# Splitting the next weights of an MoE feed-forward stage ahead of the phase and expert boundaries

## What is computed

```python
# x: (4, 2048, 1024); w1: (8, 1024, 2048); w2: (8, 2048, 1024)
xf = x.reshape(-1, D)
...
norm_g = masked / (masked + 1e-06)          # one number per token
h = gelu(einsum('nd,edh->neh', xf, w1) + b1)
y = einsum('neh,ehd->ned', h, w2) + b2
out = (y * norm_g[:, None, None]).sum(axis=1)
```

## Time and profile before

| what | us |
|---|---|
| device time, median of 2 runs | 10499.08 (10113.11 and 10885.05) |
| device time of the profiled execution | 10143.3 |
| its span on the slowest core (core 0) | 10141.3 |
| spans of the 8 cores | 10066.1 to 10141.3 |
| TensorE (matmul) busy | 8027.9, 79% of the span |
| ScalarE busy | 3868.2, 38% |
| VectorE busy | 2731.3, 27% |

### The profile page before, as it was taken

How to read it: one execution, slowest core, us unless ns; L and a number is a source line. 1 busy time by engine, 2 the same in 40 slices (tenths; PEclk the granted TensorE clock), 3 DMA queues, 4 the chain that set the end, 5 groups by cost and what they waited for, 6 DMA issues and landing times. The chain is left out here.

```text
span 10141.3 us, 83716 instructions; the slowest of 8 cores (10066.1 to 10141.3 us)
## 1 busy us (share of the span) xinstructions
PE 8027.9 (79%) x30908; PEld 3836.4 (38%) x31404; DVE 2731.3 (27%) x4507; ACT 3868.2 (38%) x3688; POOL 7.5 (0%) x15
## 2 busy tenths in 40 slices
PE   4585678898885677898896777889887676898898
PEld 2253433333332433333332333333333333343343
DVE  2213112333332112333333112333333112333332
ACT  1112003565563003565553003556554102555554
POOL 0000000000000000000000000000000000000000
PEclk7555578999997677999997667999998666999998
DMA  1000012222221111222221111222221111222222
GB/s 45 0 0 27 33 56 77 86 91 88 87 92 39 40 67 69 90 88 88 91 87 43 46 67 54 90 87 90 88 88 54 50 67 40 87 94 83 88 94 98
DMA packets 207024, 696.36 MB, mean 69 GB/s; under 512 B 29088, under 2 KB 30120, under 8 KB 206624
## 3 DMA queue, kind: packets, MB, share of 16 engines
q1 hardware_dynamic: 202048, 673.27, 19.0%
q0 software_dynamic: 4576, 17.71, 0.5%
HBM read 682.51 MB, written 8.39 MB: 68 GB/s over the span
## 5 line engine op out<-in xcount | busy, mean ns | idle before, releaser
L1172 PE MATMUL ps<-XNFH,W1SH 128*128 128x512 bf16 x4012 | 1552.8, 387 | 371.0 <-DVE W1SL L1130 363.7
L1219 PE MATMUL ps<-W2SH,H1FH 128*128 128x512 bf16 x4012 | 1559.3, 389 | 199.0 <-DVE W2SL L1151 193.9
L1174 PE MATMUL ps<-XNFL,W1SH 128*128 128x512 bf16 x4012 | 1550.3, 386 | 61.0 <-DVE W1SL L1130 56.6
L1222 PE MATMUL ps<-W2SL,H1FH 128*128 128x512 bf16 x4016 | 1560.1, 388 | 5.5 <-issue 1.4
L1229 PE MATMUL ps<-W2SH,H1FL 128*128 128x512 bf16 x4012 | 1557.0, 388 | 4.2
L1176 PE MATMUL ps<-XNFH,W1SL 128*128 128x512 bf16 x4016 | 1552.4, 387 | 5.1 <-issue 0.9
L1143 ACT ACT_TABLE_LOAD x512 | 656.9, 1283 | 1412.9 <-PE ps L1229 1411.7
L1151 DVE TENSOR_TENSOR W2SL<-W2SF,W2SH 128x1024 bf16<-128x1024 f32 x512 | 627.1, 1225 | 1984.9 <-ACT W2SH L1143 1984.9
L1187 ACT ACT_TABLE_LOAD x512 | 656.9, 1283 | 1122.9 <-PE ps L1176 1122.9
L734 PE MATMUL ps<-WSLAB,XNF 128*128 128x512 f32 x1536 | 802.9, 691 | 208.2 <-DMA WSLAB<-wq 70.1
L1172 PEld LDWEIGHTS ps<-XNFH,W1SH 128*128 128x128 bf16 x4096 | 405.4, 99 | 1060.5 <-issue 647.4
(11 more groups left out here) (180 smaller groups left out, 5004.9 us busy)
## 6 DMA issues: line engine op xcount, KB each, us to landing
W1SF<-w SPq DMA_DIRECT2D x512, 512.0 KB, 3.5
W2SF<-w SPq DMA_DIRECT2D x512, 512.0 KB, 3.5
WSLAB<-wv SPq DMA_DIRECT2D x64, 512.0 KB, 3.8
WSLAB<-wg SPq DMA_DIRECT2D x64, 512.0 KB, 3.8
WSLAB<-wo SPq DMA_DIRECT2D x64, 512.0 KB, 3.7
WSLAB<-wq SPq DMA_DIRECT2D x64, 256.0 KB, 2.7
WSLAB<-wk SPq DMA_DIRECT2D x64, 256.0 KB, 2.6
X<-x POOLq DMA_DIRECT2D x1, 8192.0 KB, 28.8
```

The costliest lines, as they stand in the source:

```text
L1172: t.matmul(ps[:, ab: ab + 512], B["W1SH"][:, half + dc * 128: half + dc * 128 + 128], XH[:, dc * 512:(dc + 1) * 512], start=(dc == 0), sto ...
L1174: t.matmul(ps[:, ab: ab + 512], B["W1SH"][:, half + dc * 128: half + dc * 128 + 128], XL[:, dc * 512:(dc + 1) * 512], start=False, stop=False)
L1219: t.matmul(ps[:, yb: yb + 512], B["H1FH"][:, hsl], B["W2SH"][:, half + dh * 512: half + dh * 512 + 512], start=(hc == 0), stop=False)
L1222: t.matmul(ps[:, yb: yb + 512], B["H1FH"][:, hsl], B["W2SL"][:, half + dh * 512: half + dh * 512 + 512], start=False, stop=False)
```

## The change

The two splitting helpers become functions of the whole stage, with their waits as arguments, and four calls move. The first two splits of w2 are emitted in phase A, behind steps 12 and 13. The first two splits of the next expert's w1 are emitted in phase B of the expert before, behind its steps 14 and 15, and so ahead of the additions into X; the waits on TensorE's no-operation go. An expert that is the first of its block has its w1 splits where they were. Because the order of the splits is no longer one phase after the other, the counts of `wvs` that TensorE and SP wait for are worked out in two tables, `w1v` and `w2v`, and the last two of the expert before are kept in `c.lw1` and `c.lw2`. The number and the shape of all instructions stay as they were.

```diff
+    def w1split(hc, dma_wait, ts_wait, val):
+        @blk.scalar
+        def _(s, hc=hc):
+            s.wait_ge(*dma_wait)
+            s.wait_ge(*ts_wait)
...
+        @blk.vector
+        def _(v, hc=hc):
+            v.wait_ge(wcs, c.wc)
...
-        wv0 = c.wv
+        W0 = c.wv
+        w1v, w2v = {}, {}
+        if pend is None:
+            w1v[0], w1v[1] = W0 + 1, W0 + 2
+            i = W0 + 2
+        else:
+            w1v[0], w1v[1] = W0 - 1, W0
...
             for hc in range(16):
-                e2.wait_ge(wvs, max(0, (wv0 - 17 + hc) if hc < 2 else (wv0 + hc - 1)))
+                e2.wait_ge(wvs, w1v[hc - 2] if hc >= 2 else c.lw1[14 + hc])
...
-        w1split(0)
-        w1split(1)
+        if pend is None:
+            w1split(0, w1_dma[0], (tsem, a_ts0), w1v[0])
+            w1split(1, w1_dma[1], (tsem, a_ts0), w1v[1])
+        pend = None
         for hc in range(16):
             @blk.tensor
-            def _(t, hc=hc, e=e, wv0=wv0):
-                t.wait_ge(wvs, wv0 + hc + 1)
+            def _(t, hc=hc, e=e, w1v=w1v):
+                t.wait_ge(wvs, w1v[hc])
...
             if hc + 2 < 16:
-                w1split(hc + 2)
-
-        w2split(0)
-        w2split(1)
+                w1split(hc + 2, w1_dma[hc + 2], (tsem, a_ts0 + hc + 1), w1v[hc + 2])
+            if hc == 12:
+                w2split(0, w2_dma[0], (ybs, c.lyb), w2v[0])
+            if hc == 13:
+                w2split(1, w2_dma[1], (ybs, c.lyb), w2v[1])
+
         for hc in range(16):
...
             if hc + 2 < 16:
-                w2split(hc + 2)
+                w2split(hc + 2, w2_dma[hc + 2], (tsem, b_ts0 + hc + 1), w2v[hc + 2])
+            if e < 7 and hc in (14, 15):
+                hcn = hc - 14
+                dw = (sqab[hcn], (c.sqa if hcn == 0 else c.sqb) + 16)
+                w1split(hcn, dw, (tsem, a_ts0 + 15 + hcn), c.wv + 1)
```

More of the change, by code:

```diff
@@ L75, in __init__ @@
         self.wv = 0
+        self.lw1 = {i: 0 for i in range(16)}
+        self.lw2 = {i: 0 for i in range(16)}
+        self.lyb = 0
 def build_program(upto="full", dbg=()):
@@ L1071, in l1_ffn_tt, with w2split, _ @@
     wcs, wvs = B["wcs"], B["wvs"]
+    ybs = B["ybs"]
+    pend = None
[4 more added lines that the diff above has]
+            s.wait_ge(*ts_wait)
+            half = (hc % 2) * 1024
+            s.copy(B["W1SH"][:, half: half + 1024],
+                   B["W1SF"][:, half: half + 1024]).then_inc(wcs, 1)
+            c.wc += 1
+        @blk.vector
+        def _(v, hc=hc):
+            v.wait_ge(wcs, c.wc)
+            half = (hc % 2) * 1024
+            v.tensor_tensor(B["W1SL"][:, half: half + 1024],
+                            B["W1SF"][:, half: half + 1024],
+                            B["W1SH"][:, half: half + 1024],
+                            ALU.subtract).then_inc(wvs, 1)
+            c.wv += 1
+            assert c.wv == val, (c.wv, val)
+    def w2split(hc, dma_wait, rd_wait, val):
+        @blk.scalar
+        def _(s, hc=hc):
+            s.wait_ge(*dma_wait)
+            s.wait_ge(*rd_wait)
+            half = (hc % 2) * 1024
+            s.copy(B["W2SH"][:, half: half + 1024],
+                   B["W2SF"][:, half: half + 1024]).then_inc(wcs, 1)
+            c.wc += 1
+        @blk.vector
+        def _(v, hc=hc):
+            v.wait_ge(wcs, c.wc)
+            half = (hc % 2) * 1024
+            v.tensor_tensor(B["W2SL"][:, half: half + 1024],
+                            B["W2SF"][:, half: half + 1024],
+                            B["W2SH"][:, half: half + 1024],
+                            ALU.subtract).then_inc(wvs, 1)
+            c.wv += 1
+            assert c.wv == val, (c.wv, val)
     for e in range(8):
@@ L1082, in l1_ffn_tt, with _ @@
         b_ts0 = a_ts0 + 16
-        wv0 = c.wv
+        W0 = c.wv
[5 more added lines that the diff above has]
+            w1v[0], w1v[1] = W0 - 1, W0
+            assert (w1v[0], w1v[1]) == tuple(pend["vals"]), (w1v, pend)
+            i = W0
+        for g in range(16):
+            if g + 2 < 16:
+                i += 1
+                w1v[g + 2] = i
+            if g == 12:
+                i += 1
+                w2v[0] = i
+            if g == 13:
+                i += 1
+                w2v[1] = i
+        for g in range(14):
+            i += 1
+            w2v[g + 2] = i
         w1_dma, w2_dma = [], []
         @blk.sync
-        def _(e2, e=e, wv0=wv0):
+        def _(e2, e=e, w1v=w1v, w2v=w2v):
             for hc in range(16):
-                e2.wait_ge(wvs, max(0, (wv0 - 17 + hc) if hc < 2 else (wv0 + hc - 1)))
+                e2.wait_ge(wvs, w1v[hc - 2] if hc >= 2 else c.lw1[14 + hc])
                 sem = sqab[hc % 2]
@@ L1102, in _ @@
             for hc in range(16):
-                e2.wait_ge(wvs, max(0, (wv0 - 1 + hc) if hc < 2 else (wv0 + 15 + hc)))
+                e2.wait_ge(wvs, w2v[hc - 2] if hc >= 2 else c.lw2[14 + hc])
                 sem = gqab[hc % 2]
@@ L1114, in _ @@
                     w2_dma.append((sem, c.gqb))
[L1116 to L1155, removed]
+        if pend is not None:
+            assert w1_dma[0] == pend["dma"][0] and w1_dma[1] == pend["dma"][1], \
+                (w1_dma[:2], pend)
         ss0 = c.ss
         vs0 = c.vs
-        w1split(0)
-        w1split(1)
+        if pend is None:
+            w1split(0, w1_dma[0], (tsem, a_ts0), w1v[0])
+            w1split(1, w1_dma[1], (tsem, a_ts0), w1v[1])
+        pend = None
         for hc in range(16):
             @blk.tensor
-            def _(t, hc=hc, e=e, wv0=wv0):
-                t.wait_ge(wvs, wv0 + hc + 1)
+            def _(t, hc=hc, e=e, w1v=w1v):
+                t.wait_ge(wvs, w1v[hc])
                 if hc == 0 and e > 0:
@@ L1232, in _ @@
                         if hc == 15 and tc == 2 and dh == 1:
-                            ii.then_inc(B["ybs"], 1)
+                            ii.then_inc(ybs, 1)
                             c.yb += 1
                 if hc == 15:
-                    ii.then_inc(B["ybs"], 1)
+                    ii.then_inc(ybs, 1)
                     c.yb += 1
@@ L1242, in l1_ffn_tt @@
             if hc + 2 < 16:
-                w2split(hc + 2)
+                w2split(hc + 2, w2_dma[hc + 2], (tsem, b_ts0 + hc + 1), w2v[hc + 2])
[3 more added lines that the diff above has]
+                w1split(hcn, dw, (tsem, a_ts0 + 15 + hcn), c.wv + 1)
+                if hcn == 0:
+                    pend = {"dma": [dw], "vals": [c.wv]}
+                else:
+                    pend["dma"].append(dw)
+                    pend["vals"].append(c.wv)
+        c.lw1 = w1v
+        c.lw2 = w2v
+        c.lyb = c.yb
         @blk.vector
         def _(v, tt=tt):
-            v.wait_ge(B["ybs"], c.yb - 1)
+            v.wait_ge(ybs, c.yb - 1)
             for tc2, dh in ((2, 0), (2, 1)):
@@ L1255, in _ @@
             c.vs += 1
-            v.wait_ge(B["ybs"], c.yb)
+            v.wait_ge(ybs, c.yb)
             for tc2, dh in ((3, 0), (3, 1), (0, 0), (0, 1), (1, 0), (1, 1)):
```

4 lines of the change are left out of this document (2 added, 2 removed).

## The result

The changed kernel is faster: its time over that of the kernel before is 0.970, with a 95% interval of 0.962 to 0.978.

What follows compares the result with a forecast made beforehand. TensorE, busy 79% of the span, and its pauses were taken as the bound: 10143.3 - 179 - 73 - 22 - 32 = 9837 us, named as 9830 for a run timed lower, range 9760 to 9925.

Steps and rivals of the forecast that it cites:

- the last of the sum: Whole kernel: 9837 us by the profiled execution, some 30 us less if timed as the lower run; 9830 named.
- Expert to expert, pauses: Phase B to next expert's phase A: the 6.5 us pause goes but for 0.1; 6.4 x 28 = 179 us.
- Rival (3): Experts' boundary: additions behind two subtractions hold TensorE; a 2.4 us slip gives back 67 us, total 9904; chance 0.09.
- Expert to expert, clock: Behind experts' boundaries: with no pause the clock stays at 1.00; 2.6 x 28 = 73 us gained.
- Phase A to phase B, pauses: Boundary 2.4 us shorter, new pause ahead of step 15 costs 1.9; 0.7 x 32 = 22 us gained, ends +29 and -43.
- Rival (2): Phase A's end: ScalarE waits for w2 loads, so the pause moves without shrinking; 43 us lost, total 9934; chance 0.10.
- Phase A to phase B, clock: Behind the boundary's shorter 3.7 us pause: less low clock, 1.0 us each, 32 us gained, ends 0 and 80.
- the row with 4.32 us: Trace row, idle 4.32 us ahead of the matmul at 1316.11 ended at clock 0.50; nearest case, saying the clock falls.
- Rival (1): Clock at the phase change: as it was, 9869; never low, 9789; within the forecast's own 0.76 chance.
- the w1 part: Next expert's early w1 splits at the experts' boundary: 179 us of pauses and 73 of clock.
- the w2 part: Early w2 splits at phase A to phase B: 22 us of pauses and 32 of clock.
- Rival (4): Feed-forward: denser matmuls bring granted clock 0.81; on half of it 620 us more, total 10457; chance 0.03.

Runs made afterwards that it cites:

- Only the w1 part: Changed kernel with the first two w2 splits back ahead of phase B; feed-forward 5920 us (5904 in the changed kernel), fastest timed execution 9843.8 us.
- only the w2 part: Changed kernel with the next expert's first two w1 splits back behind the additions into X; feed-forward 6190 us, profiled execution 10084 us.
- w2 loads earlier: Changed kernel with loads of w2 slices 0 and 1 issued ahead of w1 loads for steps 14 and 15; feed-forward 5878 us, timed 9789.6 and 9796.9.
- the densest kernel: Changed kernel with w1 copy ahead of Gelu, phase B's first step reordered, w2 splits behind steps 13 and 14; ratio to before 0.926, best 9382.1 us.
- w2 splits two steps later: Changed kernel with the first two w2 splits behind steps 14 and 15 instead of 12 and 13; feed-forward 5840 us, die 1 cores 9703 to 9713 us.
- phase B's order: Changed kernel, w2 splits behind steps 13 and 14, phase B's first step in chunk order 3, 0, 1, 2, `H1FL` wait moved; feed-forward 5656 us, ratio to before 0.945.

## Why the prediction was right, and where it was not

**The number against the medians.** The forecast of the time is wrong: 9830 us, range 9760 to 9925, against a median of 10528 over all executions. The step that failed is the last of the sum, the level that the saving is taken from: "if the changed kernel is timed as the lower run was, some 30 us less are to be expected. I name 9830". The working had two timed runs before it, 7.6% apart, and took the lower for the one that counts; nothing in the profile said so. The runs showed the other level: ten executions of the kernel before have a median of 10493.7, where the two on the table had 10499.1. Even from there the ratio would have given 10182, 3% under the 10528 measured, so over all executions together the gain does not show (1.003). What the profile supports is the ratio of like executions: 9837 / 10143.3 = 0.970, and 0.970 was measured. The sum, 9837 us, is 0.3% over what the profiled execution after took, and the four times that the result names for the changed kernel (9775 to 9861) lie in the range.

**Expert to expert, pauses: 179 us forecast, 179 measured.** Every step of it holds, down to the order of what is late next: the second subtraction, then the pair of additions, which holds TensorE for 0.07 us at the place shown (0.1 forecast). Rival (3), that the additions hold TensorE, is out: its group has 0.5 us ended by X in the whole run.

**Expert to expert, clock: 73 forecast.** The 2.6 us of one fall come from the stretch at 0.50 in the earlier trace rows (13 matmuls in 5.24 us). "Only the w1 part" measures 76 in phase A. What I left out is what this does elsewhere: the low stretches behind the pauses at the phase change, which the edit does not touch, became shorter, 30 us more. The term was priced place by place. Why one change shortens the low stretches at another place is open (see below).

**Phase A to phase B, pauses: 22 forecast, 12 to 14 measured.** (80 won ahead of B; 68 given back within A in "only the w2 part", 66 in the kernel after.) The working had the mechanism: an instruction put into a queue with 0.57 us of slack. The size of the new pause was 2.0 us instead of 1.5 to 1.9 in the mean, because the load was late in 21 places of core 0, 19.9 us in all. Rival (2), the load late everywhere, is out as a whole case (at 6.8 us everywhere it had 43 us lost), but in part it holds; "w2 loads earlier" takes 26 us of it back.

**Phase A to phase B, clock: 32 forecast, 7 measured** in "only the w2 part" (26 won, 19 lost). The clock falls behind the pause of 3.56 us at most places (240 of 256 there, 217 of 256 in the kernel after), as the row with 4.32 us said; what I took for the chance that it does not, 1.0 us of 2.5, was about right in phase B (123 x 0.21 / 32 = 0.8). But I had not asked what the new pauses of 2 to 3.5 us inside phase A do to the clock, and they cost most of it again. Rival (1) had its ends at 0 and 80; the truth lies near the first.

So the sum came out right (306 us forecast, 304 measured in the feed-forward) by luck, because two errors met: the w1 part was sized 36 us too small (252 for 288), the w2 part 36 too large (54 for 18). That shows only in the two single experiments, not in the result.

**What ScalarE's queue cost.** The 1.28 us of the table load are there again, ahead of every copy and every Gelu, and next to no time stands between: the table load of a Gelu starts 0.02 us behind the end of the copy before it (2583.16 + 1.04 = 2584.20, next load 2584.22). So the inserted copy held the queue for 2.36 us (2581.86 to 2584.22), where the working had 2.35. With the w2 load in time the pause ahead of step 15 is 1.37 us, where the working had 1.5.

**Rival (4), a lower granted clock in the feed-forward.** Not seen as an effect of the change: the feed-forward parts show 0.98 or 0.99 for 0.96 before, and in the densest kernel, the last of the experiments, core 0 has 1.00 with TensorE busy for 500.00 of 500.00 us. Two things limit this. Cores 6 and 7 of that same execution show 0.99 from 4500 to 5000 us, and their feed-forward took 5459 and 5467 us for the median of 5425. And the level of the rival does occur in a feed-forward part; core 0 of "w2 splits two steps later", a core that is not in the account:

```profile
4500.00:5000.00 500.00, 489.33 (x1855) 201.51 (x1854) 144.83 (x162) 247.24 (x223) 0.00 (x0) 0.81 0.25 81
```

That kernel's stream has more pauses than the densest one's. What brings the level in one execution and not in another isn't shown by any run.

**Low-clock matmuls without a pause.** 28 bf16 matmuls at the low clock remain in phase B where no pause stands ahead of it. All of them (234 over the eight cores of the last kernel, 251 over those of "phase B's order") lie in the last step of a block's last expert, behind the first of its 16 fp32 matmuls for `b2`. Core 1 of the last kernel:

```profile
7147.96 1.12 PE L1267 MATMUL ps<-B2S,ONESR 1*128 1x512 f32 x2
...
7150.82 0.60 PE L1270 MATMUL ps<-W2SH,H1FL 128*128 128x512 bf16 x1
...
7152.20 2.07 PE L1267 MATMUL ps<-B2S,ONESR 1*128 1x512 f32 x2
```

```profile
7100.00:7144.00 44.00, 44.00 (x206) 19.95 (x204) 10.66 (x9) 20.22 (x18) 0.00 (x0) 1.00 0.28 93
...
7151.00:7168.00 17.00, 17.00 (x26) 3.85 (x24) 0.14 (x1) 0.00 (x0) 0.00 (x0) 0.50 0.00 1
```

So the clock can fall with TensorE shown busy all the time. What went before each of these falls are the matmuls with one row of weights and one of data; that they are the cause isn't tested by a run without them.

**Open.** Why the clock stays low for 3.4 us behind some pauses and for over 5 behind others of the same length. Behind the 3.56 us of the kernel after it is 8 matmuls (3.4 us) at 88 of the 256 places and 13 or 14 (5.5 to 5.9 us) at 30. Behind 6.06 us it is 8 to 10 in 91 of 128 places of "only the w1 part" and 12 or 13 in 221 of 256 of the kernel before. So the length of the pause alone does not set it in these runs; that what went before does is not shown, since no run varies that by itself.

## What to carry to other kernels

When work of the next phase is to be moved ahead of a boundary, find in the in-order queue the last instruction that the current phase still waits for, and put the moved work just behind it: two steps earlier cost 64 us here, some 43 for the copy beyond the slack and 21 for loads that had not landed, and bought nothing, since another producer (`H1FL`) was late at the boundary anyway. Then ask of each wait that is left whether the step behind it reads what it waits for: here the first step of phase B did not, and moving that wait by a step, with the one chunk that depends on the last Gelu put last, was worth 184 us, some ten times the w2 part of the change. Price a pause with what it does to the clock behind it (behind 6.06 us idle mostly 12 or 13 matmuls of the kernel before lost 0.21 us each), price the new pauses in the same way as the old ones, and forecast a ratio, not a median, where the timed runs of one kernel lie 7% apart.

## What the hardware showed that I had not expected

- The clock can fall after the work has begun again. At the place shown, behind 3.56 us idle, three matmuls pass at 0.38 us and only the fourth is longer. Of the 256 pauses of this length on the eight cores, 86 have the first matmul longer already, 131 a later one, and at 39 the clock does not fall (4 of the 32 of core 0). Behind 6.06 us the first is longer in all 256 places of the kernel before.
- The same idle time of 6.06 us was followed mostly by 12 or 13 matmuls at the low clock in one kernel and mostly by 8 to 10 in another.
- The clock also fell to 0.50 with TensorE shown busy for 17.00 of 17.00 us, where two in five of its matmuls had a single row.
- Of three loads of 512 KB issued in a row (w1 of step 15, then two of w2) the second and third landed 5.9 and 6.7 us behind their issue in one place and 4.3 and 5.4 in another, where the median load of the run takes 3.5. On core 0 the second took 4.3 us or more and the third 5.3 or more at all 32 such places. At the slow place the first of the three was slow too (5.1 us, 3.5 at the other); why isn't shown. The slack must be set against the slow case.
- An ACT_TABLE_LOAD of 1.28 us stands ahead of each of ScalarE's copies and Gelus, with no gap behind the instruction before where its data are ready; it is part of the price of every copy (2.35 us, of which 1.04 are the copy).
